# Identity products on TensorE ahead of the one-hot sums of a four-block graph network

## The chip, the cores and the metric

The kernel runs on one core of one Trainium2 chip. The metric is the device time of one execution in microseconds (us), median of the runs shown. PE is TensorE, DVE is VectorE, ACT is ScalarE, POOL is GpSimd.

## What is computed

Four graph blocks, each with a residual and a layer norm, over 6250 nodes with 256 features and 100,000 edges. Cut to what matters:

```
x = LN(x + GAT(x))        # 2 layers, 4 heads of 64, then 1 of 64
x = LN(x + NEG_GAT(x))    # exp(-leaky_relu(.)), 2 heads of 128
x = LN(x + DOT(x))        # q.k attention, 8 heads of 32
x = LN(x + GCN(x))        # 2 layers with batch norm, widths 128 and 64

# each attention layer, per edge (src, dst):
w = exp(logit - running maximum)
out[dst] = sum(w * h[src]) / sum(w)
# each GCN layer:
out[dst] = sum(norm * h[src])
```

Each layer ends in the same thing: rows of a table are fetched by edge and summed by node.

## The kernel before, in words

The nodes are 50 windows of 128, one window per column block of an accumulator `all_acc` in on-chip memory. The edges are sorted by the window that they are summed into and cut into groups of 128. Eight groups are a batch; there are 104 batches, one per step of a loop that is written out (`for t in range(last)`).

There are six passes over the edges. `attention_pass` (L1101) makes four: **a1e** and **a2e** (kind "gat", rows of 264 and 66 values), **be** (kind "neg", 258) and **te** (kind "dot", 264). `sum_pass` (L1856) makes **g1e** and **g2e** (128 and 64 values). They are called at L2651, L2779, L2817, L2862, L2894 and L2913. a2e has other work "beside" it, the ranking for block b's order, on PE, DVE and ACT; g2e has products of its last layer beside it.

In each batch t of a pass:

- POOL issues eight indirect gathers (`gather`, L1263 and L1893), one per group, from the table in HBM into a ring of 4 batches (a1e, a2e, be), 3 (te) or 6 (g1e, g2e) in `all_Y`. A batch's slot is free when its rows have been weighed (attention) or summed (GCN) by the ring's length of batches ago.
- ACT makes the one-hot matrices: |lane - place| (L1478, L1923), then 1 - that, cut at 0 (L1484, L1926), 128 x 128 per group.
- DVE multiplies the gathered rows by the edge weights, two groups at a time (L1546, attention passes of kinds gat and neg), into `summand`.
- PE sums each group into its window: `sums` (L1318) multiplies the transposed one-hot by the rows, in float32, into one of four PSUM banks `ps_u[k % 4]`; in `sum_pass` the step (L1909) does it for eight groups into one of four bank pairs.
- DVE adds the bank to the window in `all_acc` (L1558, L1943).

The semaphores around the sum are `s_summand` (rows weighed), `s_onehot`, `s_added` (the bank's last content has been added) and `s_summed` (the sum is in the bank). In a1e and a2e PE also carries the running maximum's chain: `of_node` (L1285), `flat` (L1325), `ends` (L1333, L1334), `columns` (L1342, L1343) and `back` (L1349), each with a wait on DVE, whose scans stand at L1616 to L1646. The order of these on PE is written out by hand in `step`: of_node, sums 0 and 1, flat, sums 2 and 3, ends, sum 4, columns, sum 5, back, sums 6 and 7.

Of the kernel before, what the change touches and what calls it, by code (L numbers as in the profile page):

```python
# [13 lines left out]
P = 128  # L14
# [1086 lines left out]
def attention_pass(nc, c, stage, order, tables, table, width, acc, Y, H, C, kind, node=None, value_c0=0, queries=None, early=None, beside=None):  # L1101
# [25 lines left out]
    with ExitStack() as stack:  # L1127
# [9 lines left out]
        onehot = [m.sb(f"onehot{b}", [P, 8, P]) for b in range(2)]  # L1137
# [67 lines left out]
        with nc.Block() as block:  # L1205
# [70 lines left out]
            def _(pe):  # L1276
# [24 lines left out]
                def sums(t, b, k):  # L1301
                    if not lives(t):
                        return
                    if dot and k >= 6:
                        pe.wait_ge(s_scaled, t + 1)
                    elif dot and k >= 4:
                        pe.wait_ge(s_pooled, t + 1)
                    else:
                        pe.wait_ge(s_summand, t * BY_DVE + (k // 2 + 1))
                    if k == 0:  # L1310
                        pe.wait_ge(s_onehot, t + 1)
                        if aside:
                            pe.wait_ge(s_weight, (t + 1) * NWEIGHT)
                    if beside is None:
                        wait(pe, s_added, t * 8 + (k - 3))
                    elif k % 2 == 0:
                        wait(pe, s_added, t * 8 + (k - 2))
                    pe.matmul(ps_u[k % 4][:, 0:R], onehot[b][:, k, :], rows[:, t % RING, k, WEIGHT0:value_c0 + HC] if dot else summand[:, b, k, :], start=True, stop=True).then_inc(s_summed, 1)  # L1318

                def flat(t, b):  # L1320
# [535 lines left out]
def sum_pass(nc, c, stage, order, table, width, acc, spare, beforehand=None):  # L1856
# [4 lines left out]
    with ExitStack() as stack:  # L1861
# [19 lines left out]
        with nc.Block() as block:  # L1881
# [19 lines left out]
            def _(pe):  # L1901
                def step(t):
                    r, u, b = t % RING, t % AHEAD, t % MARKS
                    pe.wait_ge(s_onehot, t + 1)
                    wait(pe, s_added, (t - AHEAD + 1) * 8)
                    for k in range(8):
                        if k % 4 == 0:
                            pe.wait_ge(s_rows[r][k // 4], t // RING * 64 + 64)
                        last = pe.matmul(ps_u[u][:, k * width:(k + 1) * width], onehot[b][:, k, :], rows[:, r, k, :], start=True, stop=True)  # L1909
                    last.then_inc(s_summed, 1)  # L1910
                    if window_at(t, 0) is not None:
                        early.turn(pe, window_at(t, 0))
                    if window_at(t, 1) is not None:
                        early.product(pe, window_at(t, 1))
# [1044 lines left out]
```

## Time and profile before

| | us |
|---|---|
| median of 3 runs | 10409.85 |
| lowest, highest | 10393.64, 10424.56 |
| the profiled execution, its own time | 10424.9 |
| span of the profiled execution | 10423.2 |
| PE busy | 6055.0 (58%), 32739 instructions |
| DVE busy | 5838.2 (56%) |
| ACT busy | 4570.6 (44%) |
| POOL busy | 5885.3 (56%) |
| mean granted clock of PE | 0.706 |

A float32 matmul shows as two records, called passes here: the 832 sums of a stage are 1664 records. The granted clock is in parts of full speed: 1.00 is 2.4 GHz and 0.50 is 1.2 GHz. In the lists of groups, what stands behind the last bar is the idle time of the engine ahead of the group and what ended most of it; "issue" is time with nothing to wait for that the profile shows, and "remote" is a semaphore whose sender the profile could not name. A wait for several semaphores is put down to the one that came last by the profile.

### The profile page before, as it was taken

How to read it: one execution, taken by the hardware profiler on the slowest of the kernel's cores; microseconds unless marked ns; L12 is line 12 of the kernel's file. 1: busy time of each engine (PE TensorE's matmuls, PEld its weight loads, DVE VectorE, ACT ScalarE, POOL GpSimd, SP SyncE). 2: the span in 40 equal slices, each digit the busy share in tenths (PEclk: the TensorE clock that was granted, in tenths of full speed). 3: DMA queues.
4: the chain of work that ended last, by engine and by line, in shares of the span. 5: the costliest groups of instructions: out<-in, count | busy, mean ns of one | idle time of the engine just before them, and what ended most of it. 6: DMA issues, size and time to landing. Idle time of an engine off the chain costs nothing. (4 is left out here: it accounts for less than half of the span.)

```text
span 10423.2 us, 138279 instructions
## 1 busy us (share of the span) xinstructions
PE 6055.0 (58%) x32739; PEld 4141.4 (40%) x32739; DVE 5838.2 (56%) x17354; ACT 4570.6 (44%) x14076; POOL 5885.3 (56%) x6036
## 2 busy tenths in 40 slices
PE   5775566666556656565555567888873323333434
PEld 3443344444433333343333334555553222323333
DVE  8997566666555555564544568899982212211113
ACT  6996222222344444443222226777753323223332
POOL 7996455554444444425666615666655666466664
PEclk8998666666566666667666688899886555555556
DMA  1332333332222222223333325666641111111111
GB/s 52 117 105 87 107 100 98 97 99 82 61 64 64 66 74 64 62 68 103 107 107 106 107 90 167 177 181 181 179 132 45 47 46 47 40 26 23 23 24 37
DMA packets 518562, 902.79 MB, mean 87 GB/s; under 512 B 149378, under 2 KB 258844, under 8 KB 517404
## 3 DMA queue, kind: packets, MB, share of 16 engines
q0 software_dynamic: 226304, 550.69, 20.1%
q1 hardware_dynamic: 291484, 343.26, 10.8%
q8 instruction: 305, 5.00, 0.2%
q14 instruction: 469, 3.84, 0.1%
HBM read 820.41 MB, written 73.07 MB: 86 GB/s over the span
## 5 line engine op out<-in xcount | busy, mean ns | idle before, releaser
L1263 POOL DMA_INDIRECT all_Y<-table,all_row x3328 | 3212.0, 965 | 2817.5 <-DVE all_Y L1546 1482.1
L1893 POOL DMA_INDIRECT all_Y<-table,all_row x1664 | 1570.0, 943 | 825.0 <-issue 488.2
L1318 PE MATMUL be_ps_u<-all_Y,be_onehot 128*128 128x258 f32 x1664 | 669.8, 539 | 511.3 <-issue 260.9
L1909 PE MATMUL g1e_ps_u<-all_Y,g1e_onehot 128*128 128x128 f32 x1664 | 364.4, 351 | 830.7 <-issue 746.0
L1318 PE MATMUL a1e_ps_u<-all_Y,a1e_onehot 128*128 128x264 f32 x1664 | 788.1, 609 | 48.6 <-DVE all_acc L1558 47.6
L1943 DVE TENSOR_TENSOR all_acc<-all_acc,g1e_ps_u 128x128 f32 x832 | 238.8, 287 | 966.8 <-DMA all_window<-kept_window_dst 745.9
L1558 DVE TENSOR_TENSOR all_acc<-all_acc,be_ps_u 128x258 f32 x832 | 350.8, 422 | 604.2 <-remote 395.2
L1318 PEld LDWEIGHTS be_ps_u<-all_Y,be_onehot 128*128 128x128 f32 x1664 | 377.5, 258 | 755.0 <-issue 650.1
L1909 PEld LDWEIGHTS g1e_ps_u<-all_Y,g1e_onehot 128*128 128x128 f32 x1664 | 317.5, 261 | 877.6 <-issue 810.2
L1318 PE MATMUL te_ps_u<-all_Y,te_onehot 128*128 128x264 f32 x1664 | 586.6, 463 | 97.1 <-DVE all_Y L1538 59.8
L1943 DVE TENSOR_TENSOR all_acc<-all_acc,g2e_ps_u 128x64 f32 x832 | 183.5, 221 | 817.9 <-DMA table<-g2l_tile 383.1
L1318 PE MATMUL a2e_ps_u<-all_Y,a2e_onehot 128*128 128x66 f32 x1664 | 375.8, 363 | 448.7 <-DVE all_acc L1558 344.9
L1909 PE MATMUL g2e_ps_u<-all_Y,g2e_onehot 128*128 128x64 f32 x1664 | 309.8, 325 | 481.7 <-issue 454.5
L717 ACT ACTIVATE all_X<-all_Y,all_acc 128x128 f16<-128x128 f16 x784 | 239.6, 387 | 718.6 <-DVE all_acc L701 660.7
L747 PE MATMUL a2e_rank_ps_p<-all_X 128*128 128x512 f16 (+1 forms) x1568 | 545.2, 509 | 1.1 <-issue 0.9
L1297 PE MATMUL te_ps_q<-all_X,te_turned 128*128 x1664 | 490.1, 432 | 65.6 <-DVE te_product L1601 42.2
L1318 PEld LDWEIGHTS a2e_ps_u<-all_Y,a2e_onehot 128*128 128x128 f32 x1664 | 312.4, 262 | 515.5 <-issue 499.2
L649 POOL TENSOR_SCALAR all_acc<-all_Y,all_acc 128x128 f16<-128x128 f16 x392 | 488.8, 1258 | 45.4 <-DVE all_acc L636 35.4
L1909 PEld LDWEIGHTS g2e_ps_u<-all_Y,g2e_onehot 128*128 128x128 f32 x1664 | 313.0, 259 | 490.1 <-issue 471.1
L1318 PEld LDWEIGHTS a1e_ps_u<-all_Y,a1e_onehot 128*128 128x128 f32 x1664 | 424.1, 288 | 139.8 <-DVE all_Y L1546 52.1
L1484 ACT ACTIVATE be_onehot<-be_distance 128x1024 f32<-128x1024 f16 x104 | 109.9, 1057 | 842.0 <-PE be_ps_u L1318 739.2
L1926 ACT ACTIVATE g1e_onehot<-g1e_distance 128x1024 f32<-128x1024 f16 x104 | 109.9, 1057 | 815.5 <-DMA all_window<-kept_window_dst 752.0
(568 smaller groups left out, 16478.9 us busy)
## 6 DMA issues: line engine op xcount, KB each, us to landing
all_Y<-table,all_row POOLq DMA_INDIRECT x4992
a1e_place_row<-places_dst SPq DMA_DIRECT2D x104, 256.0 KB
a2e_place_row<-places_dst SPq DMA_DIRECT2D x104, 256.0 KB
be_place_row<-places_src SPq DMA_DIRECT2D x104, 256.0 KB
te_place_row<-places_src SPq DMA_DIRECT2D x104, 256.0 KB
all_Y<-lows_dst SPq DMA_DIRECT2D x98, 256.0 KB
all_Y<-codes_dst SPq DMA_DIRECT2D x98, 256.0 KB
all_acc<-lows_src SPq DMA_DIRECT2D x98, 256.0 KB
```

The costliest lines, as they stand in the source:

```text
L649: pool.tensor_scalar(self.row1[b][:, k, :], self.kept.half16, self.row[b][:, k:k + 1], self.kept.other_t[:, t * 8 + k:t * 8 + k + 1], ALU. ...
L717: act.activation(self.row1[b][:, k, :], self.kept.half16, ACT.Sign, bias=self.row[b][:, k:k + 1]).then_inc(self.s_valued, 1)
L747: last = pe.matmul(ps[:, 0:a1 - a0], self.row1[b][:, k, :], self.column1[b][:, k, a0:a1], start=first, stop=final)
L1263: pool.indirect_dma_start(out=rows[:, r, k, :], out_offset=None, in_=table, in_offset=bass.IndirectOffsetOnAxis(ap=order.row[:, t * 8 + k: ...
L1297: last = pe.matmul(ps_q[pair % 2][:, j * HC:(j + 1) * HC], turned[b][:, k * P:(k + 1) * P], queries[:, bass.ds(windows.at(windows_j, chunk ...
L1318: pe.matmul(ps_u[k % 4][:, 0:R], onehot[b][:, k, :], rows[:, t % RING, k, WEIGHT0:value_c0 + HC] if dot else summand[:, b, k, :], start=Tr ...
L1484: act.activation(onehot[b][:, :, :], distance[:, :, :], ACT.Relu, scale=-1.0, bias=1.0).then_inc(s_onehot, 1)
L1558: dve.tensor_tensor(mine, mine, ps_u[k % 4][:, 0:R], ALU.add).then_inc(s_added, 1)
L1893: pool.indirect_dma_start(out=rows[:, r, k, :], out_offset=None, in_=table, in_offset=bass.IndirectOffsetOnAxis(ap=order.row[:, t * 8 + k: ...
L1909: last = pe.matmul(ps_u[u][:, k * width:(k + 1) * width], onehot[b][:, k, :], rows[:, r, k, :], start=True, stop=True)
L1926: act.activation(onehot[t % MARKS][:, :, :], distance[:, :, :], ACT.Relu, scale=-1.0, bias=1.0).then_inc(s_onehot, 1)
L1943: dve.tensor_tensor(mine, mine, ps_u[(t - 1) % AHEAD][:, k * width:(k + 1) * width], ALU.add).then_inc(s_added, 1)
```

## The change

In `sums` the wait on `s_added` moves from behind the waits on `s_summand` and `s_onehot` to ahead of them. Between it and them PE makes products of the 128 x 128 float32 identity with itself, into columns 0 to 127 of the bank that the real sum is about to fill: two in a1e and be, one in a2e, none in te. In the GCN passes the wait on the gathered rows stays first, and four products per group follow it, with the identity as weights and the group's one-hot (128 or 64 columns of it) moving, into the group's own slice. The real sum starts its bank anew, so that it overwrites them.

```diff
@@ sums, in attention_pass
                     if not lives(t):
                         return
+                    if beside is None:
+                        wait(pe, s_added, t * 8 + (k - 3))
+                    elif k % 2 == 0:
+                        wait(pe, s_added, t * 8 + (k - 2))
+                    for _ in range(0 if dot else 1 if beside is not None else 2 if gat else 2):
+                        pe.matmul(ps_u[k % 4][:, 0:P], c.ident[:, :], c.ident[:, :], start=True, stop=True)
                     if dot and k >= 6:
                         pe.wait_ge(s_scaled, t + 1)
...
-                    if beside is None:
-                        wait(pe, s_added, t * 8 + (k - 3))
-                    elif k % 2 == 0:
-                        wait(pe, s_added, t * 8 + (k - 2))
@@ step on PE, in sum_pass
                         if k % 4 == 0:
                             pe.wait_ge(s_rows[r][k // 4], t // RING * 64 + 64)
-                        last = pe.matmul(ps_u[u][:, k * width:(k + 1) * width], onehot[b][:, k, :], rows[:, r, k, :], start=True, stop=True)
+                        to = ps_u[u][:, k * width:(k + 1) * width]
+                        for _ in range(4):
+                            pe.matmul(to, c.ident[:, :], onehot[b][:, k, 0:width], start=True, stop=True)
+                        last = pe.matmul(to, onehot[b][:, k, :], rows[:, r, k, :], start=True, stop=True)
                     last.then_inc(s_summed, 1)
```

That is 1664 added products in a1e, 832 in a2e, 1664 in be, 3328 each in g1e and g2e: 10,816 in all. No other engine's instructions change. The line numbers move by 2 in `sums` (L1318 becomes L1320, and the dummies are L1309) and to L1913 (dummies) and L1914 (sum) in `sum_pass`.

PE in one step of a1e, before (`a1e_ps_u` are the four banks of the sums, `ps_l` and `ps_r` those of the running maximum's chain, x2 is two alike in a row):

```order
L1285 MATMUL a1e_ps_n<-all_node_parts,a1e_turned 128x24
L1318 MATMUL a1e_ps_u<-all_Y,a1e_onehot 128x264 x2
L1325 MATMUL a1e_ps_l<-all_ident,a1e_joined 36x128
L1318 MATMUL a1e_ps_u<-all_Y,a1e_onehot 128x264 x2
L1333 MATMUL a1e_ps_r<-all_ident,a1e_local 1x36 x2
L1334 MATMUL a1e_ps_r<-a1e_row_peak,all_ones 1x4
L1318 MATMUL a1e_ps_u<-all_Y,a1e_onehot 128x264
L1342 MATMUL a1e_ps_r<-all_ones,a1e_row_peak 36x1 x2
L1343 MATMUL a1e_ps_l<-a1e_fall,a1e_onehot 128x4
L1318 MATMUL a1e_ps_u<-all_Y,a1e_onehot 128x264
L1349 MATMUL a1e_ps_r<-all_ident,a1e_peak 128x36
L1318 MATMUL a1e_ps_u<-all_Y,a1e_onehot 128x264 x2
```

And of the change:

```order
L1285 MATMUL a1e_ps_n<-all_node_parts,a1e_turned 128x24
L1309 MATMUL a1e_ps_u<-all_ident 128x128 x2
L1320 MATMUL a1e_ps_u<-all_Y,a1e_onehot 128x264
L1309 MATMUL a1e_ps_u<-all_ident 128x128 x2
L1320 MATMUL a1e_ps_u<-all_Y,a1e_onehot 128x264
L1327 MATMUL a1e_ps_l<-all_ident,a1e_joined 36x128
L1309 MATMUL a1e_ps_u<-all_ident 128x128 x2
L1320 MATMUL a1e_ps_u<-all_Y,a1e_onehot 128x264
L1309 MATMUL a1e_ps_u<-all_ident 128x128 x2
L1320 MATMUL a1e_ps_u<-all_Y,a1e_onehot 128x264
L1335 MATMUL a1e_ps_r<-all_ident,a1e_local 1x36 x2
```

Every sum has two products ahead of it, and what stood behind a sum (flat, ends, columns) now stands behind three instructions for each one.

PE in g2e, around the first product of the last layer's work beside it (L1833, L1835 in the change; `ps_t` is that work's bank), before:

```order
L1909 MATMUL g2e_ps_u<-all_Y,g2e_onehot 128x64 x8
L1833 MATMUL g2e_ps_t<-all_ident,all_X 128x128 x2
L1909 MATMUL g2e_ps_u<-all_Y,g2e_onehot 128x64 x8
L1848 MATMUL g2e_ps_o<-gf_W,g2e_turned 128x256 x2
L1849 MATMUL g2e_ps_o<-gf_W,all_Y 128x256
L1909 MATMUL g2e_ps_u<-all_Y,g2e_onehot 128x64 x8
```

And of the change:

```order
L1914 MATMUL g2e_ps_u<-all_Y,g2e_onehot 128x64
L1835 MATMUL g2e_ps_t<-all_ident,all_X 128x128 x2
L1913 MATMUL g2e_ps_u<-g2e_onehot,all_ident 128x64 x4
L1914 MATMUL g2e_ps_u<-all_Y,g2e_onehot 128x64
L1913 MATMUL g2e_ps_u<-g2e_onehot,all_ident 128x64 x4
L1914 MATMUL g2e_ps_u<-all_Y,g2e_onehot 128x64
```

Four products of the identity with the group's one-hot come ahead of each sum, so that a batch has 40 matmuls where it had 8; g1e is the same without the products beside it.

## Rows read from the trace of the kernel before

**Rows 1.** Windows: one per pass (a1e, a2e, be, te, g1e, g2e), three inside g1e.

Columns: window in us, its length, busy us (x instructions) of PE, PE's loads, DVE, ACT and POOL, mean PEclk, DMA share, GB/s.

```profile
1160.00:2590.00 1430.00, 937.20 (x3890) 588.38 (x3889) 921.86 (x2763) 410.68 (x1330) 759.55 (x798) 0.64 0.35 96
2720.00:4610.00 1890.00, 1124.08 (x8610) 737.21 (x8609) 1028.21 (x4245) 868.61 (x2806) 793.69 (x814) 0.63 0.26 64
4770.00:6050.00 1280.00, 734.71 (x2466) 443.04 (x2466) 640.63 (x1644) 378.40 (x1135) 778.52 (x817) 0.69 0.39 106
6330.00:7720.00 1390.00, 1138.94 (x4725) 777.83 (x4724) 1255.15 (x2776) 1044.72 (x3187) 922.88 (x911) 0.89 0.61 176
7880.00:9060.00 1180.00, 362.41 (x1648) 315.63 (x1648) 229.41 (x800) 357.44 (x919) 780.17 (x827) 0.57 0.18 46
9130.00:10310.00 1180.00, 449.11 (x2004) 405.25 (x2003) 191.66 (x843) 365.74 (x966) 779.26 (x826) 0.58 0.12 23
8200.00:8233.00 33.00, 4.96 (x15) 3.73 (x13) 4.01 (x14) 4.47 (x13) 22.80 (x25) 0.50 0.20 50
7900.00:7903.00 3.00, 2.05 (x8) 1.78 (x8) 0.00 (x0) 0.00 (x0) 2.29 (x3) 0.50 0.17 44
8193.60:8196.60 3.00, 3.00 (x28) 2.90 (x26) 0.66 (x4) 2.94 (x8) 2.21 (x3) 1.00 0.17 45
```

**Rows 2.** The gathers' line on POOL in a1e, a2e, be, g1e and g2e.

x count: shortest/median/longest ns, first and last start in us.

```profile
L1263 POOL DMA_INDIRECT all_Y<-table,all_row x832: 940/946/1241, 1108.4 to 2555.1; - x167
...
L1263 POOL DMA_INDIRECT all_Y<-table,all_row x832: 938/944/1323, 2695.8 to 4572.6; - x167
...
L1263 POOL DMA_INDIRECT all_Y<-table,all_row x832: 940/946/1200, 4750.5 to 6031.0; - x167
...
L1893 POOL DMA_INDIRECT all_Y<-table,all_row x832: 938/944/1045, 7873.8 to 9047.8; - x167
...
  DMA all_window<-kept_window_dst: 145.2, 41
...
L1893 POOL DMA_INDIRECT all_Y<-table,all_row x832: 938/944/992, 9122.5 to 10299.4; - x167
```

**Rows 3.** Timeline of POOL in g1e, 8225 to 8238.

Columns: start us, busy us, engine, line, operation, out<-in, [idle before <-releaser].

```profile
8235.74 0.94 POOL L1893 DMA_INDIRECT all_Y<-table,all_row  x1 [5.63 <-DMA all_window<-kept_window_dst]
8236.99 0.94 POOL L1893 DMA_INDIRECT all_Y<-table,all_row  x1 [0.30 <-issue]
```

**Rows 4.** Timeline of DVE in g1e, 8186 to 8222.
```profile
8218.75 3.30 DVE L1943 TENSOR_TENSOR all_acc<-all_acc,g1e_ps_u 128x128 f32 x8 [16.24 <-DMA all_window<-kept_window_dst]
```

**Rows 5.** Timelines in be, 5343 to 5366: PE, DVE, POOL.
```profile
5348.61 1.31 PE L1318 MATMUL be_ps_u<-all_Y,be_onehot 128*128 128x258 f32 x4 [0.24 <-issue]
5360.95 1.70 PE L1318 MATMUL be_ps_u<-all_Y,be_onehot 128*128 128x258 f32 x3 [11.02 <-DVE all_acc L1558]
...
5360.38 0.42 DVE L1558 TENSOR_TENSOR all_acc<-all_acc,be_ps_u 128x258 f32 x1 [10.68 <-remote]
...
5362.19 0.94 POOL L1263 DMA_INDIRECT all_Y<-table,all_row  x1 [4.36 <-DVE all_Y L1546]
```

**Rows 6.** Groups by line: DVE's additions in g1e and be, a scan in a2e.

Columns: out<-in, shapes, xcount | busy us, mean ns | idle before, us, and its releasers.

```profile
L1943 DVE TENSOR_TENSOR all_acc<-all_acc,g1e_ps_u 128x128 f32 x832 | 238.8, 287 | 966.8 <-DMA all_window<-kept_window_dst 745.9
L1558 DVE TENSOR_TENSOR all_acc<-all_acc,be_ps_u 128x258 f32 x832 | 350.8, 422 | 604.2 <-remote 395.2
...
L1626 DVE TENSOR_TENSOR_SCAN a2e_row_forward<-a2e_turns,a2e_ps_r 1x18 f32<-1x18 f32 x103 | 18.3, 178 | 422.7 <-remote 408.5 <-issue 13.6 <-PE a2e_ps_r L1334 0.6
```

**Rows 7.** Groups by line: the one-hot sums of a1e, be and te.
```profile
L1318 PE MATMUL be_ps_u<-all_Y,be_onehot 128*128 128x258 f32 x1664 | 669.8, 539 | 511.3 <-issue 260.9
...
L1318 PE MATMUL a1e_ps_u<-all_Y,a1e_onehot 128*128 128x264 f32 x1664 | 788.1, 609 | 48.6 <-DVE all_acc L1558 47.6
...
L1318 PE MATMUL te_ps_u<-all_Y,te_onehot 128*128 128x264 f32 x1664 | 586.6, 463 | 97.1 <-DVE all_Y L1538 59.8
```

**Rows 8.** Timeline of DVE at the end of a1e, one scan a step.
```profile
2562.74 0.41 DVE L1621 TENSOR_TENSOR_SCAN a1e_local<-a1e_flags,a1e_forward 36x128 f32<-36x128 bf16 x1
...
2572.46 0.41 DVE L1621 TENSOR_TENSOR_SCAN a1e_local<-a1e_flags,a1e_forward 36x128 f32<-36x128 bf16 x1
```

## The prediction, made blind

> **What bounds the kernel now.** I read the windows of the six passes first, then the line of the gathers on POOL, then the timelines of single steps, and last the lines of the matmul that the change works on.
>
> The windows show no engine full in the five passes that the change touches [rows 1]: PE is busy 937 of 1430 us in a1e, 1124 of 1890 in a2e, 735 of 1280 in be, and 362 and 449 of 1180 in g1e and g2e, at a mean granted clock of 0.57 to 0.69. Only te, which the change leaves alone, has PE busy 1139 of 1390 us, at 0.89. POOL is busy 760 to 794 us in each of the five.
>
> The gathers say how fast a pass could be [rows 2, 3]. One takes 0.944 us and the next follows 0.30 us later, so 8 gathers are 10.0 us of a batch. Over 831 intervals that is 1039 us. From first start to last start the passes take 1447 (a1e), 1877 (a2e), 1281 (be), 1174 (g1e) and 1177 us (g2e). The excess over the queue's own pace is 408, 838, 242, 135 and 138 us, **1761 us together**: all that the change can act on.
>
> What makes the excess is visible in g1e. Every fourth batch or so POOL stops for want of a free ring slot (here 5.63 us, [rows 3]; 145.2 us in 41 stops over the pass, as much as its whole excess, [rows 2]). PE can be dense here: 28 passes in the 3.00 us from 8193.60, at clock 1.00. In the 33 us from 8200 it made 15, at clock 0.50 [rows 1], while POOL went on without a pause. The profile names no operand that PE lacks there. DVE then stands 16.24 us until a sum is complete [rows 4]; the releaser named there is a DMA long done, so it is PE. In be the same thing shows as 10.68 us of DVE on "remote" and 11.02 us of PE's sums behind it, and POOL's next gather comes 4.36 us late [rows 5]. I call such a stretch, in which PE creeps while gathers run, a **hold**. Holds are most of the idle time of the consumers: 745.9 us ahead of the additions in g1e, 395.2 in be, 408.5 ahead of one scan in a2e [rows 6].
>
> **The change, part by part.** (1) It adds 10,816 products. Each is two passes (832 sums of the old kernel are 1664 passes in every row), so 21,632 passes: 3328 in a1e, 1664 in a2e, 3328 in be, 6656 each in g1e and g2e, none in te. A pass of 128 columns takes 3.00/28 = 0.107 us at full clock, its load of weights beside it, and at half clock at most 2.05/8 = 0.26 us (the two windows of 3 us, [rows 1]). I use 0.11, and twice the 0.107, 0.21, at half clock. g2e's dummies have 128 columns of weights and 64 moving; I price them alike, which is an upper bound.
>
> Per batch the added PE time is then:
> - a1e and be: 32 passes, 3.5 us at full clock, 6.7 at half.
> - a2e: 16 passes, 1.8 or 3.4 us.
> - g1e and g2e: 64 passes beside the 16 real ones, so 80 in all: 8.8 us at full clock, 16.8 at half. The gathers' pace is 10.0 us.
>
> At full clock all of it fits beside the gathers. In a1e the idle time of PE is 493 us of 1430, 4.8 us a batch, and the dummies take 3.5; in be it is 545 us, 5.3 a batch; in a2e 766 us, 7.5 a batch against 1.8. So the first-order cost is **0 us, hidden under the 10.0 us of gathers**. If that cover is gone (half clock) it is 6.8 us a batch in g1e and g2e, the slower rival below.
>
> A sentence on a rule. The window with 28 passes in 3.00 us at full clock [rows 1] has 26 loads in 2.90 us in the same stretch, so load and product overlap. The Trainium skill, "TensorE: Matmul & The Clock Gate", section "Part 3: Packing small matmuls", says that a load overlaps matmuls in flight only when its row group differs; by that, load and product of a dummy would come one after the other, and the dummies would cost about twice what I take. The trace disagrees; the measurement decides, and what is left of the case is the second half of the slower rival.
>
> (2) What it removes: idle time of PE at low clock. a1e and te make the same product, 264 columns, and a pass has 609 ns in a1e and 463 in te [rows 7]; 1664 x 0.146 = 243 us of PE time in a1e that a clock like te's would give. For be, 539 against 463, it is 126 us. Of PE's time only what the chain DVE-PE-DVE waits for reaches the end; PE stands before these passes for 48.6 us only in a1e. I take half: 120 and 60 us. In g1e and g2e the gathers set the end and the clock alone gives nothing.
>
> (3) What the change may do to the holds. No row of the kernel before shows dense PE work of this sort in the five passes, so I bound it from both sides. From below: nothing (in be the hold begins 0.2 us after a dense run of sums, [rows 5], so that dense work by itself does not keep it off). From above: the whole excess in be, g1e and g2e; in a1e a step takes 9.7 us once the last gather has started at 2555.1 [rows 8], against 1447/104 = 13.9 before, and 9.7 is under the 10.0 of the gathers, so again the whole excess; and in a2e the 408.5 us of the scan's wait. te is the nearest row: PE 82% busy at clock 0.89 while more gathered bytes land than anywhere (0.61 DMA share), and few holds. The change brings the others toward te's state, which speaks for the upper half; te's own gaps show that it will not be all. I take 0.8 of the excess in g1e and g2e, where four products per sum make PE 88% busy (8.8 of 10.0); 0.6 in be and a little under 0.5 in a1e, with two; and a third of the 408.5 in a2e, with one:
> a1e -190, a2e -150, be -140, g1e -110, g2e -105: **-695 us**. The clock's share (180) is within a1e's and be's terms.
>
> (4) The s_added wait moves ahead of the summand wait. It is for a bank freed three sums earlier, mostly met by then; the real sum waited for both before anyway. 0 us. What is queued behind the dummies on PE are flat, ends, columns and back of the scan chain: at most one group of two dummies, 4 passes, 0.44 us at full clock, stands before each; four such places x 104 batches would be 183 us if all were exposed. In a1e DVE's chain of scans is not on the gathers' path as long as the step stays near 10.0, so I charge it nothing and keep it for the range.
>
> Sum: 10,424.9 - 695 = 9730 on the profiled execution; the median of the runs lies 15 us under it, so **9715 us**.
>
> **The rivals.**
> - *Only the clock rises, holds stay.* Gain 100 to 250 by the halves and wholes of (2), less what the scan chain loses: about 10,230. For it: be's hold began in dense work. Against it: te. Chance 0.20.
> - *All holds go.* 408 + 408 + 242 + 135 + 138 = 1331: about 9080. Chance 0.08.
> - *It does nothing*: dummies run only in PE's idle time, and that idle time at "issue" is not PE's to fill, so that they merely pass through. 10,410 within 30. Chance 0.06.
> - *Slower: dummies creep too.* PE takes its work in order, so in a hold the 64 dummies of a g batch creep like the real passes (15 in 33 us, [rows 1]) or run at half clock: 16.8 us a batch against 11.3 now. Loads that stand ahead of the dummies' products instead of beside them would come to the same: 80 x (0.107 + 2.90/26) = 17.5 us. Two passes x 104 x 5.5 = +1144 us: about 11,550. It decides from a mean spacing above 11.3/80 = 0.141 us. The mean clock of g1e is 0.57 now, for it; that PE is idle 70% of the time there explains this clock, against it, as does te, whose clock is 0.89 at 82% busy. Chance 0.16, of which 0.02 for the loads. The Trainium skill, same page, section "What's actually happening", has the idle state as the throttled one and activity as what releases it; the clocks in [rows 1] agree.
>
> **The numbers.** A measurement tells about 0.3%, 31 us, from no change. Likeliest case 0.50, with its own range 9250 to 10,130: at the one end the 1331 us less 0.4 of a2e's 408, at the other the clock's 180 and half of the g passes' 273 less the 35 that the scan chain may lose. Faster: 0.50 + 0.20 + 0.08 = 0.78; same 0.06; slower 0.16. The range takes in the clock-only, the do-nothing and the all-holds case, and leaves the slower one out: 9050 to 10,440.
>
> **What would show it.** Right: clock above 0.85 in all six windows; first to last gather near 1060 us in g1e and g2e, POOL's 145.2 us of stops down to under 30; DVE's "remote" wait in be under half; a te window unchanged. Wrong: a mean clock near 0.6 in g1e with PE over 90% busy (slower rival); clock up but the stops still there (clock alone); a1e longer with DVE waiting for ps_r and ps_l lines (the scan chain behind dummies).

## The result, and the profile after

| | before | change |
|---|---|---|
| median, us | 10409.38 (4 runs) | 11476.11 (4 runs) |
| lowest, highest | 10393.64, 10424.56 | 11452.3, 11497.18 |
| span of the profiled execution | 10423.2 | 11495.4 |
| PE busy, records | 6055.0, 32739 | 8764.1, 54371 |
| mean granted clock | 0.706 | 0.78 |

The ratio is **1.1028**, 95% interval 1.1006 to 1.1051: 10% slower, where 7% faster was forecast. The time lies outside the range and 74 us under the slower rival's.

One sentence is needed for all that follows: the same kernel before takes 10.4 to 10.5 ms on some chips and 8.70 ms on others, each time within 0.5%, and the result on record, as the profile of before, is from the first kind. I call them places with holds and places without. Each ratio below is against the kernel before on the same chip. A pass's time is from one profile, and where it is set against a profile from another chip the text says so if it matters.

The length of a pass is taken from its first gather's start to its last addition's end:

| pass | before | change | difference | forecast |
|---|---|---|---|---|
| a1e | 1491 | 1804 | +313 | -190 |
| a2e | 1920 | 1942 | +22 | -150 |
| be | 1311 | 1377 | +65 | -140 |
| te | 1441 | 1437 | -4 | 0 |
| g1e | 1202 | 1303 | +101 | -110 |
| g2e | 1204 | 1778 | +574 | -105 |

The sum is +1071 us of the 1072 between the spans. The expectations further down take the last two passes of the change some 10 us too short (1294 and 1768, +92, +564, together 656). Windows of the change, one per pass in the same order (columns as in [rows 1]):

```profile
1160.00:2900.00 1740.00, 1236.50 (x7163) 984.67 (x7162) 928.35 (x2761) 411.15 (x1327) 757.17 (x799) 0.76 0.29 80
3080.00:4940.00 1860.00, 1299.30 (x10121) 954.20 (x10120) 1014.26 (x4186) 859.67 (x2780) 763.32 (x785) 0.70 0.26 64
5150.00:6440.00 1290.00, 948.89 (x5558) 807.28 (x5557) 621.51 (x1590) 360.07 (x1090) 746.75 (x788) 0.84 0.37 102
6740.00:8120.00 1380.00, 1144.56 (x4697) 784.08 (x4697) 1258.77 (x2765) 1040.30 (x3167) 919.99 (x908) 0.88 0.61 177
8350.00:9560.00 1210.00, 1044.93 (x8065) 997.92 (x8065) 231.71 (x808) 344.48 (x883) 732.44 (x777) 0.94 0.16 43
9700.00:11380.00 1680.00, 1636.62 (x8450) 1606.27 (x8449) 194.28 (x855) 351.98 (x932) 731.93 (x776) 0.59 0.08 16
```

The clock did rise in four of the five passes (0.64 to 0.76, 0.63 to 0.70, 0.69 to 0.84, 0.57 to 0.94), and not in g2e, 0.58 to 0.59, although PE is busy for 97% of that window. te is as before.

The page's groups of the change, and the gathers' line with its waits in g1e and g2e:

```profile
L1913 PE MATMUL g2e_ps_u<-g2e_onehot,all_ident 128*128 128x64 f32 x6656 | 1386.9, 376 | 83.0 <-issue 72.2
L1913 PE MATMUL g1e_ps_u<-g1e_onehot,all_ident 128*128 128x128 f32 x6656 | 1005.4, 290 | 182.6 <-issue 166.7
...
L1560 DVE TENSOR_TENSOR all_acc<-all_acc,be_ps_u 128x258 f32 x832 | 350.0, 421 | 667.7 <-remote 331.1
...
L1320 PE MATMUL a1e_ps_u<-all_Y,a1e_onehot 128*128 128x264 f32 x1664 | 634.1, 470 | 0.0
```

```profile
L1895 POOL DMA_INDIRECT all_Y<-table,all_row x832: 938/944/1045, 8272.3 to 9524.1; - x167
...
  PE g1e_ps_u L1914: 242.1, 97
...
L1895 POOL DMA_INDIRECT all_Y<-table,all_row x832: 938/944/992, 9621.0 to 11334.4; - x167
...
  PE g2e_ps_u L1914: 706.0, 98
```

The additions in be still wait 331.1 us on "remote" (395.2 before, [rows 6]). A pass of a1e's sums is as fast as te's (470 ns, 463 in [rows 7]), as forecast, and a1e is 313 us longer all the same.

Where a1e grew shows on DVE, at the scan that reads the product of `ends`, before and in the change:

```profile
L1626 DVE TENSOR_TENSOR_SCAN a1e_row_forward<-a1e_turns,a1e_ps_r 1x72 f32<-1x72 f32 x104 | 29.9, 288 | 58.8 <-remote 52.4 <-PE a1e_ps_r L1334 5.6
L1628 DVE TENSOR_TENSOR_SCAN a1e_row_forward<-a1e_turns,a1e_ps_r 1x72 f32<-1x72 f32 x104 | 30.3, 292 | 339.3 <-remote 332.6 <-PE a1e_ps_r L1336 4.2 <-issue 2.0
```

That is 280 of the 313 us. (Ahead of all four operations of DVE that read the chain's products the idle time grew from 441 to 727 us.) The scan waits for nothing of PE's but this product (`s_ends`), and it starts 3.4 us in the mean behind the end of the product's record, against 0.7 before and 0.1 in the change in a place without holds (e6 below). So DVE does not stand there because the product is queued behind dummies: PE has made it.

In g1e POOL now stops once a batch, 97 times and 242.1 us, where it stopped 41 times for 145.2 us [rows 2].

What a stop looks like now, on PE and on POOL, in g1e:

```profile
8905.35 1.06 PE L1913 MATMUL g1e_ps_u<-g1e_onehot,all_ident 128*128 128x128 f32 x8
...
8906.47 0.50 PE L1913 MATMUL g1e_ps_u<-g1e_onehot,all_ident 128*128 128x128 f32 x3
8907.65 0.27 PE L1913 MATMUL g1e_ps_u<-g1e_onehot,all_ident 128*128 128x128 f32 x1 [0.68 <-issue]
8908.35 0.39 PE L1913 MATMUL g1e_ps_u<-g1e_onehot,all_ident 128*128 128x128 f32 x2 [0.43 <-issue]
8909.05 0.39 PE L1913 MATMUL g1e_ps_u<-g1e_onehot,all_ident 128*128 128x128 f32 x2 [0.31 <-issue]
```

```profile
8906.45 0.94 POOL L1895 DMA_INDIRECT all_Y<-table,all_row  x1 [0.30 <-issue]
8909.94 0.94 POOL L1895 DMA_INDIRECT all_Y<-table,all_row  x1 [2.54 <-PE g1e_ps_u L1914]
```

PE makes 8 passes in 1.06 us until a batch's last gather is on its way, then starts come 0.70 us apart (8907.65, 8908.35, 8909.05), with no operand missing, and it is dense again when POOL has been quiet for some 1.7 us. A batch takes 12.1 us: 10.0 of gathers and the stop. The hold has not shrunk away; it has become shorter and comes in nearly every batch.

In g2e the clock shows in the length of the groups of eight:

```profile
9810.57 1.91 PE L1913 MATMUL g2e_ps_u<-g2e_onehot,all_ident 128*128 128x64 f32 x8
...
9812.70 2.02 PE L1850 MATMUL g2e_ps_o<-gf_W,g2e_turned 128*128 128x256 f32 x4
9814.51 0.83 PE L1851 MATMUL g2e_ps_o<-gf_W,all_Y 128*128 128x256 f32 x2
...
9816.24 1.06 PE L1913 MATMUL g2e_ps_u<-g2e_onehot,all_ident 128*128 128x64 f32 x8
...
9823.75 0.22 PE L1913 MATMUL g2e_ps_u<-g2e_onehot,all_ident 128*128 128x64 f32 x1 [0.18 <-issue]
9824.45 0.32 PE L1913 MATMUL g2e_ps_u<-g2e_onehot,all_ident 128*128 128x64 f32 x1 [0.49 <-issue]
...
9827.03 1.81 PE L1913 MATMUL g2e_ps_u<-g2e_onehot,all_ident 128*128 128x64 f32 x8
```

Eight dummies take 1.91 us at 9810 (1.2 GHz), 1.06 behind the 256-column products at L1850 and L1851 (2.4 GHz), and 1.81 again behind the trickle of 9823 to 9825. Ahead of this rise PE is busy for the whole 90 us from 9720 to 9810 with 64-column products, at 1.2 GHz:

```profile
9720.00:9810.00 90.00, 90.00 (x414) 88.92 (x413) 9.49 (x42) 17.98 (x48) 37.74 (x40) 0.50 0.08 15
```

### The profile page after: what moved, and what is told of

It is laid out like the page before. It is cut to its first block and busy times, and to the rows that moved or that the text cites. A ratio compares the mean times of both kernels' runs of the same rounds, so it can differ in the third digit from the quotient of the medians.

```text
span 11495.4 us, 179576 instructions
## 1 busy us (share of the span) xinstructions
PE 8764.1 (76%) x54371; PEld 7148.0 (62%) x54371; DVE 5852.2 (51%) x17354; ACT 4565.4 (40%) x14076; POOL 5873.5 (51%) x6036
## 5 line engine op out<-in xcount | busy, mean ns | idle before, releaser
L1913 PE MATMUL g2e_ps_u<-g2e_onehot,all_ident 128*128 128x64 f32 x6656 | 1386.9, 376 | 83.0 <-issue 72.2
L1913 PEld LDWEIGHTS g2e_ps_u<-g2e_onehot,all_ident 128*128 128x128 f32 x6656 | 1322.7, 291 | 92.4 <-issue 85.2
L1913 PE MATMUL g1e_ps_u<-g1e_onehot,all_ident 128*128 128x128 f32 x6656 | 1005.4, 290 | 182.6 <-issue 166.7
L1913 PEld LDWEIGHTS g1e_ps_u<-g1e_onehot,all_ident 128*128 128x128 f32 x6656 | 897.0, 204 | 222.0 <-issue 219.8
L1309 PE MATMUL be_ps_u<-all_ident 128*128 128x128 f32 x3328 | 626.6, 319 | 356.3 <-DVE all_acc L1560 209.2
L1309 PEld LDWEIGHTS be_ps_u<-all_ident 128*128 128x128 f32 x3328 | 577.7, 226 | 477.3 <-DVE all_acc L1560 247.7
L1309 PE MATMUL a2e_ps_u<-all_ident 128*128 128x128 f32 x1664 | 504.0, 392 | 269.9 <-DVE all_acc L1560 188.5
L1309 PE MATMUL a1e_ps_u<-all_ident 128*128 128x128 f32 x3328 | 690.6, 342 | 8.8 <-DVE all_acc L1560 8.8
L1560 DVE TENSOR_TENSOR all_acc<-all_acc,be_ps_u 128x258 f32 x832 | 350.0, 421 | 667.7 <-remote 331.1
L1320 PE MATMUL te_ps_u<-all_Y,te_onehot 128*128 128x264 f32 x1664 | 590.9, 467 | 103.6 <-DVE all_Y L1540 72.2
L1320 PE MATMUL a1e_ps_u<-all_Y,a1e_onehot 128*128 128x264 f32 x1664 | 634.1, 470 | 0.0
L1309 PEld LDWEIGHTS a1e_ps_u<-all_ident 128*128 128x128 f32 x3328 | 589.3, 239 | 70.4 <-DVE all_acc L1560 10.6
L1320 PE MATMUL be_ps_u<-all_Y,be_onehot 128*128 128x258 f32 x1664 | 581.7, 436 | 0.0
L1309 PEld LDWEIGHTS a2e_ps_u<-all_ident 128*128 128x128 f32 x1664 | 347.5, 256 | 325.7 <-DVE all_acc L1560 228.0
```

Of the source, the lines that this page charges most:

```text
L1309: pe.matmul(ps_u[k % 4][:, 0:P], c.ident[:, :], c.ident[:, :], start=True, stop=True)
L1560: dve.tensor_tensor(mine, mine, ps_u[k % 4][:, 0:R], ALU.add).then_inc(s_added, 1)
L1913: pe.matmul(to, c.ident[:, :], onehot[b][:, k, 0:width], start=True, stop=True)
```

## The experiments

**The first four**, where there were no holds (before 8697.22 us, 25 runs). The wait alone moved:

```diff
-                    for _ in range(0 if dot else 1 if beside is not None else 2 if gat else 2):
+                    for _ in range(0):
...
-                        for _ in range(4):
-                            pe.matmul(to, c.ident[:, :], onehot[b][:, k, 0:width], start=True, stop=True)
```

> Only the s_added wait is moved, no dummies anywhere. Both theories: the real sum waited for both before, so nothing: 10,410 within 30 us. If the order of the two waits mattered by itself, a1e and be would show it, in which PE's mean wait for the additions is largest.

8701.36 us, ratio 1.0003 (0.9994 to 1.0013). The moved wait is nothing, there.

Dummies in g1e and g2e alone (only the first of those two lines changed):

> Four dummies a group in g1e and g2e, none in the attention passes (the waits stay moved). In the profile of the change these two passes grew by 92 and 564 us from first gather to last addition. If the passes are independent of each other: 10,410 + 656 = 11,066 within 40. If part of the growth came from what the earlier passes leave behind (queues, clock), less than 600 more.

8705.73 us, 1.0017 (1.0006 to 1.0028): not 656 us, but 9 by the medians. In g1e the profile has, in 1000 us,

```profile
6500.00:7500.00 1000.00, 943.33 (x8009) 908.83 (x8008) 229.53 (x800) 340.98 (x874) 756.25 (x801) 1.00 0.20 54
```

8009 passes at clock 1.00 beside gathers at their own pace (801 in 1000 us). This is what term (1) had worked out: 80 passes in 8.8 of 10.0 us. It is true where there are no holds.

128 columns in g2e's dummies:

```diff
+                        wide = ps_u[u][:, k // 2 * 2 * width:k // 2 * 2 * width + P] if width < P else to
+                        for _ in range(4 if width == P else 8 if k % 2 == 0 else 0):
+                            pe.matmul(wide, c.ident[:, :], onehot[b][:, k, :], start=True, stop=True)
```

> The change, but in g2e the dummies move all 128 columns of the one-hot into two groups' slices (eight ahead of every second sum, so as many dummies as in the change and twice the columns). Theory A, the clock: g2e's dummies of 64 columns did not raise the clock (0.59 at 97% busy), and passes of 128 would, as in g1e (0.94); then a pass is spaced 0.111 us instead of 0.213, and g2e falls from 1768 to about 1330 us: in all 11,476 - 440 = 11,040. Theory B, the count of instructions: they are as many as before, so g2e stays near 1768 us and the total near 11,476.

8700.15 us, 1.0002 (0.9993 to 1.0012): neither number, since the growth was not there to be taken away. POOL's pause:

```diff
+                    if not dot and t > 0:
+                        apart(pool, s_rows[(t - 1) % RING], (t - 1) // RING * 128 + 128, s_passed)
...
+                    if t > 0:
+                        wait(pool, s_rows[(t - 1) % RING][1], (t - 1) // RING * 64 + 64)
```

> The kernel before, and one thing added: before it issues the gathers of a batch, POOL waits until those of the batch before have landed (a1e, a2e, be, g1e, g2e). Theory C: PE's holds begin when gathers follow each other without a pause for some 8 to 10 us, and end when POOL pauses; then a pause of about 2 us a batch takes the holds away, DVE's waits on remote all but vanish, a2e falls from 18.1 us a batch to under 15 and a1e from 13.9 to about 12.5: 10,410 - 320 - 150 = 9,940, with g1e and g2e near 12 us a batch (+50 each): about 10,000. Theory D: the holds are due to something on PE itself (its instructions, its clock), and a pause only adds its own 2 us a batch where gathers bound the pass (be, g1e, g2e +100 to +200 each) and nothing elsewhere: 10,600 to 10,900.

10060.93 us, 1.1568 (1.1549 to 1.1588) of 8697: the bare price of the pauses. Its passes: a1e 1425, a2e 1584, be 1319, g1e 1256, g2e 1248 us. It could tell nothing of holds, as there were none.

**The change again**, and without its dummies in g1e and g2e, where there were no holds either:

> The change itself again, beside the kernel before. In the last four runs the kernel before took 8697 us where it had taken 10,410, its passes ran at the gathers' own 10.0 us a batch, and the holds were gone. Theory E: the holds belong to the place where a program runs (which chip or core, where its memory lies), and the change costs only where they are; without holds it is 8697 within 1% (the sum passes alone were 1.0017), with holds 11,476 against 10,410 as on record. Rival: the change costs by its array time in a1e and be whatever the place; then even without holds a1e grows by 100 us or more (3328 passes of 0.111 us beside 1664 real ones of 0.22, at a step of 10.3 us of which PE was busy 8.3).

> The change without the dummies of g1e and g2e. Without holds: as the kernel before within 1%. With holds: 10,410 + 400 = 10,810, from the growth of a1e (313), be (65) and a2e (22) in the profile of the change.

8706.96 us against 8700.35, 1.001 (1.000 to 1.002), and 8700.74, 0.9998 (0.9988 to 1.0009). Theory E stands, its rival falls: a1e takes 1100 us with the dummies, as it did in the first run of this section without them. The windows of the change there, a1e, a2e, be and g1e:

```profile
1160.00:2200.00 1040.00, 968.87 (x7075) 767.79 (x7073) 905.22 (x2727) 406.63 (x1316) 757.83 (x791) 1.00 0.48 132
2340.00:3520.00 1180.00, 1015.02 (x10176) 776.81 (x10174) 1018.99 (x4209) 855.00 (x2782) 856.67 (x804) 0.92 0.40 102
3700.00:4710.00 1010.00, 852.13 (x5636) 731.52 (x5635) 630.50 (x1613) 373.00 (x1105) 761.53 (x803) 0.94 0.48 132
6500.00:7500.00 1000.00, 943.61 (x8010) 908.93 (x8009) 229.64 (x801) 340.92 (x874) 755.91 (x802) 1.00 0.19 54
```

The clock is near 1, PE is busy most of the time, and no pass is longer. So the dummies' array time at the full clock is not the cost on record.

**Kind and number of dummies**, where there were holds (before 10515.44 us, 3 runs). Neither the kernel before nor the change was profiled on this chip. The passes below are set against the profiles of the result's chip, where before took 106 us less, so some of each growth over before belongs to the chip. Few passes of many columns, in bf16:

```diff
+                    for _ in range(0 if dot else 1):
+                        pe.matmul(ps_u[k % 4][:, 0:256 if beside is not None else 512], c.ident16[:, :],
+                                  bc(c.ident16[:, :].rearrange("p (a n) -> p a n", a=1), [P, 2 if beside is not None else 4, P]), start=True, stop=True)
...
+                        for _ in range(0 if k * width % 512 else 8 if width == P else 16):
+                            pe.matmul(ps_u[u][:, k * width:k * width + 512], c.ident16[:, :], bc(c.ident16[:, :].rearrange("p (a n) -> p a n", a=1), [P, 4, P]), start=True, stop=True)
```

> Few dummies of many columns in place of many of 128: in bf16, one of 512 columns ahead of each sum in a1e and be (256 in a2e), 16 of 512 a batch in g1e and g2e. In a1e it is 832 passes in place of 3328, at about half the time on PE; in g1e 1664 in place of 6656. Where the holds are (the kernel before at 10,410): by the theory that each pass costs because PE's passes trickle in a hold (singles at multiples of 0.70 us), a1e returns from 1804 to about 1500 us, g1e from 1294 to 1200, g2e from 1768 to 1250, in all near 10,450 or below, with the clock above 0.85. By the theory of array time alone a1e falls by half of its 313 only, to 1650, and the total is near 10,750. Where they are not (8697): within 0.3% of 8697 by both, hidden under the gathers.

10638.57 us, 1.0116 (1.0081 to 1.0151). a1e 1591, be 1337, g1e 1228, g2e 1239 us. The mean clock of g1e and g2e is 0.72 and 0.76, against 0.57 and 0.58 before, and under the 0.85 that was expected. So a good part of the clock is to be had for 1.2% rather than 10%, and still nothing comes back for it. a1e lies between the two theories' numbers (at most +100 of the +313).

One column:

```diff
+                        pe.matmul(ps_u[k % 4][:, 0:1], c.ident[:, :], c.ident[:, 0:1], start=True, stop=True)
...
+                            pe.matmul(to[:, 0:1], c.ident[:, :], onehot[b][:, k, 0:1], start=True, stop=True)
```

> As many dummies as in the change, each moving one column in place of 128 or 64. Where the holds are: if the number of passes is what costs, a1e stays near 1800 us and g1e near 1290; if array time, a1e and g1e fall back to 1491 and 1202 within 60. Clock: stays near the kernel before (0.57 in g1e) by both. Where the holds are not: 8697 within 0.3%, clock 0.50 in g1e.

12375.42 us, 1.1768 (1.1733 to 1.1802): slower than the change itself, which neither theory had. a1e 1834, be 1514, g1e 1830, g2e 1911 us. Windows of a1e and g1e:

```profile
1200.00:2900.00 1700.00, 1673.86 (x6925) 1305.56 (x6925) 898.19 (x2670) 397.97 (x1287) 737.26 (x778) 0.50 0.29 79
9000.00:9400.00 400.00, 400.00 (x1877) 400.00 (x1876) 54.44 (x190) 82.86 (x213) 175.50 (x186) 0.50 0.11 31
```

PE is busy all 400 us with 1877 passes, 0.213 us each, at 1.2 GHz: a one-column pass takes here what a 128-column one takes at that clock, and its load is 128 columns of weights as before. 80 x 0.213 = 17.0 us a batch, and g1e's additions come 17.07 us apart. This is the slower rival's sum, in a kernel that it was not made for.

Five and seven dummies a group:

```diff
-                        for _ in range(4):
+                        for _ in range(5 if width == P else 7):
```

> Five dummies a group in g1e and seven in g2e, the rest as in the change. PE then has 96 and 128 passes a batch: 10.7 and 14.2 us at 0.1115 us each, over the gathers' 10.0. Where the holds are not: g1e grows by 0.7 x 104 = 70 us and g2e by 4.2 x 104 = 440 us: 9200 in all; the cover ends at 10.0 / 0.1115 = 90 passes. Where the holds are: the same and the trickle on top, g1e at 14 us a batch (1450 us) and g2e above 2300.

12871.12 us, 1.2239 (1.2203 to 1.2274). g1e 1603 us, 14.8 us a batch for 96 passes; g2e 2813 us, 26.5 a batch for 128 (128 x 0.213 = 27.3). In g1e 16 more passes than in the change are 1.8 us of array time at the full clock and cost 2.9 (1603 - 1303 = 300 us over 104).

**e4, e5 and e1 again, and half the dummies**, in a place without holds again (before 8711.83 us, 18 runs), though meant for one with them.

> The kernel of e4 (g2e's dummies move 128 columns), meant for a place with holds. There, if the half clock is what made g2e grow (in the profile of the change its clock falls in each trickle and comes back only with the 256-column products of the last layer, while in g1e passes of 128 columns bring it back within some us): g2e falls from 1768 to about 1330 us, 11,476 - 440 = 11,040. If the number of passes alone: g2e stays at 1768. Where there are no holds, as e4: same as the kernel before.

> The kernel of e5 (POOL waits once a batch until the last batch's gathers have landed), meant for a place with holds. Theory C (holds need gathers without a pause): the passes take what they took in e5, a1e 1425, a2e 1584, be 1319, g1e 1256, g2e 1248 us, and the total is 10,061 + 30, so faster than the kernel before there (10,410 to 10,515). Theory D (holds come from elsewhere): each pass takes its time of before plus the pauses, a2e 1920 or more, in all above 10,700.

> The kernel of e1 (only the s_added wait moved). With holds or without: within 0.3% of the kernel before. If the moved wait had a part in a1e's +313 us, a1e would show it here.

8712.25 us (1.0002, 0.9991 to 1.0014), 10083.13 (1.1574, 1.154 to 1.1607) and 8708.18 (1.0001, 0.999 to 1.0013): as the first time. The moved wait was not measured by itself where there are holds. e15 and e16 below bear on it there: a1e has pauses and no dummies in both, with the wait moved in e15 and unmoved in e16, and takes 1352 and 1354 us.

```diff
-                    for _ in range(0 if dot else 1 if beside is not None else 2 if gat else 2):
+                    for _ in range(0 if dot else 1):
...
-                        for _ in range(4):
+                        for _ in range(2):
```

> Half the dummies in a1e, be (one), g1e and g2e (two), a2e as in the change. Where the holds are, if the cost is linear in the passes: a1e +156, be +33, g1e +46, g2e +282 of the change's, total +540. If it starts only when PE's work of a batch no longer fits the time between two holds, far less than half: in g1e (48 passes, 5.3 us at full clock, 10.2 at half) nothing at full clock and +100 at half. Where they are not: nothing.

8741.99 us, 1.0035 (1.0017 to 1.0053): a little slower, where nothing was expected. It is a1e, 1127 us against 1100. Its clock is 0.85 there, against 1.00 with two dummies a sum; but with none it is 0.75 (e1) at 1100 us, so the clock alone does not explain the 27 us.

**Two questions in one kernel**, since neither had been answered where there are holds: pauses in a1e, a2e, be and g1e, no dummies but g2e's, of 128 columns.

```diff
+                    if not dot and t > 0:
+                        apart(pool, s_rows[(t - 1) % RING], (t - 1) // RING * 128 + 128, s_passed)
...
-                    for _ in range(0 if dot else 1 if beside is not None else 2 if gat else 2):
+                    for _ in range(0):
...
+                    if width == P and t > 0:
+                        wait(pool, s_rows[(t - 1) % RING][1], (t - 1) // RING * 64 + 64)
...
-                        for _ in range(4):
-                            pe.matmul(to, c.ident[:, :], onehot[b][:, k, 0:width], start=True, stop=True)
+                        wide = ps_u[u][:, k // 2 * 2 * width:k // 2 * 2 * width + P] if width < P else to
+                        for _ in range(8 if width < P and k % 2 == 0 else 0):
+                            pe.matmul(wide, c.ident[:, :], onehot[b][:, k, :], start=True, stop=True)
```

> One kernel for two questions, read pass by pass. In a1e, a2e, be and g1e there are no dummies, and POOL waits once a batch until the last batch's gathers have landed, as in e5. In g2e there is no such wait, and the dummies of the change move 128 columns, as in e4. Where the holds are: by theory C (holds need gathers without a pause) a1e takes about 1425 us, a2e 1584, be 1319 and g1e 1256, as where there are none; by theory D each takes its time of before and the pauses on top (a2e 1920 or more). g2e: about 1330 us if the half clock made it grow to 1768, 1768 if the number of passes alone did. Where the holds are not: those times for the first four, and 1047 us for g2e.

There were holds (before 10396.02 us, 9 runs). The kernel took 10353.11 us in the median of 8, spread from 10065.4 to 10430.89, so only its passes are read, from the profile of one of the longer executions (10396.25 us); which pass gave the shortest its time is not known. g2e 1373 us; a1e 1352, a2e 1790, be 1322, g1e 1261. Its g2e:

```profile
9100.00:10250.00 1150.00, 1003.63 (x7535) 952.51 (x7534) 173.71 (x763) 321.83 (x851) 677.19 (x716) 0.93 0.11 21
```

Clock 0.93 in place of 0.59, with the number of dummies as in the change and twice the columns, and 405 of the 574 us are gone. The dummies also stand eight ahead of every second sum here, and the passes ahead of g2e have pauses; e18 below has those pauses with 64-column dummies, and g2e at 0.60 and 1702 us. **The half clock is shown as the larger part of g2e's growth**, by one profile. The remaining 169 us, at 0.93, are nearer to the 101 by which g1e grew at 0.94. Theory C's times come out for be and g1e. a1e is 139 us shorter than before, though the pauses are added, but also 73 us under the 1425 that the same pauses give without holds, which theory C does not explain. a2e is 130 us shorter where 336 were expected.

**Pauses where they gained**, and a second one in a2e:

```diff
+                    if gat and t > 0:
+                        apart(pool, s_rows[(t - 1) % RING], (t - 1) // RING * 128 + 128, s_passed)
...
+                        if beside is not None and k == 4:
+                            pool.wait_ge(s_rows[r], t // RING * 128 + 64)
```

> The kernel before with pauses in a1e and a2e alone: once a batch in both, and in a2e once more at the middle of the batch, so that never more than four gathers follow each other there. Where the holds are (before near 10,400): a1e 1352 us as in the last run (1491 before); a2e, if holds need five or more gathers on end, near 15.3 us a batch, 1600 us (1920 before), in all 10,400 - 140 - 320 = 9,940; if a2e's time is set by something else (the ranking's work on PE and DVE), near 1790, in all 10,130. Where there are no holds (8700): a1e +320 as in e5, a2e +360 or more, in all 9,380 or more, slower.

10063.9 us against 10403.5, **0.9667** (0.9649 to 0.9685): faster than both kernels where there are holds. a1e 1354, a2e 1723 us. The gathers' line in a1e (first start to last 1324 us, 1447 in [rows 2]):

```profile
L1267 POOL DMA_INDIRECT all_Y<-table,all_row x832: 943/949/1242, 1108.7 to 2432.6; - x167
...
  DMA all_Y<-table,all_row: 281.4, 99
...
  DVE all_Y L1550: 19.1, 50
```

POOL waits 281.4 us for landings, by the edit, and 19.1 us for rows to be weighed, where it waited 426.8 before. The late products are not all gone: DVE's idle time ahead of the scan of `ends` is 0.9 us (58.8 before), but ahead of the scan of `flat` it is 209.6 (62.6 before). This kernel was not run where there are no holds; the pauses of e5 alone cost a1e 325 us there, so it would be slower.

**The change with the pauses**, first in a place without holds, then in one with them:

> The change, with POOL's pause once a batch in all five passes. If the dummies cost because of the holds, they cost nothing once these are gone: a1e 1354 within 40, be 1320, g1e 1256, the last at a clock near 1.00, and g2e 1250 if its clock comes up and 1770 if it stays at half. If they cost by standing ahead of the scan chain on PE, a1e is at 1354 + 200 or more also with pauses. Where the kernel before has no holds (8700): a1e 1425 as in e5, both ways less telling.

> The kernel of e17 again, meant for a place with holds (before near 10,400). If the dummies cost because of the holds: a1e 1354 within 40 us, be 1320, g1e 1256 (the times of e15). If they cost by standing ahead of the scan chain on PE: a1e at 1354 + 200 or more.

The first took 10125.53 us, 1.1638 (1.1597 to 1.1678) of 8702; a1e 1414, g2e 1281. The second, one run with holds, took 11279.09 against 10390.12. Its be has 1332 and its g1e 1278 us, as without dummies (1322, 1261): there the dummies cost next to nothing once POOL pauses. But a1e has 1782 us, not 1354, and g2e 1702 at clock 0.60. In a1e DVE waits for a product that PE has long made; PE, POOL and DVE of one step:

```profile
1997.05 0.19 PE L1338 MATMUL a1e_ps_r<-a1e_row_peak,all_ones 1*1 1x4 f32 x2
...
2004.19 0.36 PE L1346 MATMUL a1e_ps_r<-all_ones,a1e_row_peak 1*36 1x1 f32 x4 [5.86 <-DVE a1e_fall L1640]
```

```profile
2000.09 0.94 POOL L1265 DMA_INDIRECT all_Y<-table,all_row  x1 [0.30 <-issue]
2011.09 0.94 POOL L1265 DMA_INDIRECT all_Y<-table,all_row  x1 [10.06 <-DVE all_Y L1550]
```

```profile
2002.57 0.29 DVE L1630 TENSOR_TENSOR_SCAN a1e_row_forward<-a1e_turns,a1e_ps_r 1x72 f32<-1x72 f32 x1 [5.12 <-remote]
```

By its record L1338 ends at 1997.24; the scan that needs it starts at 2002.57, 1.5 us after POOL's last gather ended (2001.03). DVE's idle time ahead of this scan is 307.9 us over the pass, as in the change and not as in e16. The hold is back although POOL pauses: it pauses 10 us, at another point of the step. So the dummies in a1e cost where there are holds (430 us over e15 here, nothing in e17 over e5) and a pause a batch does not undo it. Theory C is too simple for a1e.

## Why the prediction was wrong

*The views were read right in the main, up to the word "cover".* The holds, the pass times (0.111 and 0.213 us, start to start) and the clock's rise in four passes came out. So did the excess: without holds the five passes take 1060, 1183, 1043, 1038 and 1038 us from first to last gather (e1), so 1594 of the 1761 us go with the holds. Two readings were loose: POOL's 41 stops in 104 batches are one in 2.5 and not in four, and a third of a2e's 408.5 us is 136 and not the 150 of the sum. Neither matters for the sign. Four steps failed.

**Term (1), "the first-order cost is 0 us, hidden under the 10.0 us of gathers".** The idle time of PE was counted as free, 818 of 1180 us in g1e. Most of it could be filled (PE is busy 1045 of 1210 us in the change), but the part of it that is a hold could not: 15 passes in 33 us [rows 1]. The row was on the page, and I used it for the mechanism and not for the cover. A batch of g1e before needs 16 passes, and between holds PE made nearly three batches of them in one burst and let POOL run ahead:

```profile
8190.15 6.54 PE L1909 MATMUL g1e_ps_u<-all_Y,g1e_onehot 128*128 128x128 f32 x43 [0.32 <-issue]
```

With 80 passes a batch, 8.9 us at the full clock, there is next to nothing left to catch up with. PE is late for the ring in 97 of 104 batches, and POOL's stops for it grow from 145.2 to 242.1 us: that is the +101 us. Without holds the term is right (e2, e6).

**Term (3), "what the change may do to the holds", -695 us.** There is no such gain. te was the nearest row, and I took its dense PE for the cause of its few holds. te's gathers are also broken by 143 waits for PE, and e15 and e16 speak for this as the likelier cause, though te itself was not tried: without any dummies, breaking up the gathers shortens a1e by 139 us; with dummies and no breaks it grows by 313. What I read as evidence against, that in be a hold began behind a dense run [rows 5], was right, and should have stopped the step.

**The clock in g2e.** Term (1) takes "at full clock all of it fits" for g2e too. I priced a 64-column pass as an upper bound by the 128-column one. Its spacing is the same, 0.111 or 0.213 us by the clock, but the clock that g2e ran at was the lower one. The change keeps PE busy for 97% of g2e at a mean of 0.59, and e15 puts 405 of 574 us on that. Without holds too the first 45 us of g2e differ, 64 columns (the change, e6) and 128 (e4), but the change then rises and stays up (third line, e6):

```profile
7555.00:7600.00 45.00, 34.97 (x163) 34.96 (x164) 2.37 (x11) 20.29 (x55) 31.25 (x34) 0.50 0.17 39
```

```profile
7555.00:7600.00 45.00, 41.34 (x339) 40.72 (x340) 6.51 (x29) 24.85 (x66) 34.02 (x37) 0.92 0.13 28
```

```profile
7600.00:7700.00 100.00, 100.00 (x855) 98.73 (x853) 20.39 (x91) 37.58 (x99) 75.62 (x81) 0.99 0.13 28
```

So 64-column passes do run at 2.4 GHz once the clock is up. Where there are holds it does not stay up. In g2e of the change the granted clock rises 28 times; 27 times it falls again behind a trickle in which PE stood idle for 1.2 to 1.9 us (at 9825 in the lines of g2e above), and it can then stay low for long, from 9719 to 9815 with PE busy. The 28th rise comes after the last gather, and lasts to the end of the pass. So the holds cost here by way of the clock.

**The slower rival** gave 11,550, and 11,476 was measured; it was given 0.16. It is right for g2e (+572 worked out, +574 measured), and its turning point of 0.141 us lies between the two spacings. For g1e it is wrong (+572, +101), since there the clock rose. And it had nothing for a1e, which grew by 313. The total is near by these errors cancelling, which is luck.

**Term (4)**, that dummies ahead of the scan chain cost nothing, fails where there are holds and stands where there are none. The forecast's own sign for it, a1e longer with DVE waiting for ps_r, came, but not for the reason that it gave: the product had been made, and its completion reached DVE 3.4 us late in the mean. Why dummies make the completions of `ends` late there, and which part the clock has in it, is open.

**The load rule** of the Trainium skill ("TensorE: Matmul & The Clock Gate", "Part 3: Packing small matmuls") would have had load and product of a dummy in turn. The 8009 passes of e2, busy 943 of 1000 us beside loads busy 909, disagree again: the two overlap. The section "What's actually happening" on the same page of the Trainium skill says that activity releases the throttle. The trace agrees in g1e (0.57 to 0.94), and does not in g2e with holds: 97% busy at 0.59.

## What to carry to other kernels

Idle time on an engine is cover only if the engine could have worked in it: look in the timeline at what it does there before giving it work. Where fill work is to change TensorE's clock, try its shape and read the granted clock stretch by stretch: here, with holds, 128-column dummies ran at 0.94, 64-column ones at 0.59 (0.99 without holds) and one-column ones at 0.50 with PE full, and one wide bf16 product in place of several cost 1.2% and not 10%, at 0.72 to 0.76. When an engine waits for a product, compare its start with the end of the product's record: the product may be long made. And run a change on more than one chip before believing a stall in its profile: this one's 10% is 0.1% elsewhere.

## What the hardware showed that was not expected

- The same program takes 8.70 ms on two of the chips used and 10.39 to 10.52 ms on four others, with all of the difference in the six passes with indirect gathers (a2e 701 us, te 67). What sets the places apart was not found.
- Where there are holds, PE's starts in g1e come at multiples of 0.70 us while gathers follow each other (in before at 8201.14, 8203.24, 8206.03 and 8208.14: 3, 4 and 3 times 0.70), and a product's completion can reach DVE 5 us late. Whether this is the supply of instructions, the semaphores, or something else, no run here tells. The packets of the instruction queue take about as long in both places, 1.1 us in the median in g1e before and 1.0 in e1, 13 in each.
- A wait of POOL for the last batch's landing, once a batch, takes 139 us off a1e there (e15) and adds 325 us where there are no holds (e5).
